# Product with V in pairs of steps, the sums leaving their bank in halves, and VectorE's remainder inside the even steps

## What is computed

```python
c_q = x @ Wq_down
c_kv = x @ Wkv_down
q_c = (c_q @ Wq_up).reshape(b, s, N_HEADS, HEAD_DIM)      # 128 heads of 4
q_r = (x @ Wq_rope).reshape(b, s, N_HEADS, ROPE)          # 128 heads of 64
k_c = (c_kv @ Wk_up).reshape(b, s, N_HEADS, HEAD_DIM)
v_c = (c_kv @ Wv_up).reshape(b, s, N_HEADS, HEAD_DIM)
k_r = x @ Wk_rope
scores = (einsum('bqhd,bkhd->bhqk', q_c, k_c) + einsum('bqhd,bkd->bhqk', q_r, k_r)) / scale
out = einsum('bhqk,bkhd->bqhd', softmax(scores), v_c)
s = out.reshape(b, s, N_HEADS * HEAD_DIM) @ Wo
...
xn = _layernorm(x)                                        # x: 8 x 256 x 512
x = x + attention(xn) * silu(ffn(xn))
```

## Time and profile before

| | us |
|---|---|
| median of 3 runs | 2015.23 |
| lowest, highest | 2010.91, 2015.4 |
| the profiled execution | 2011.28 |
| its span, first to last instruction | 2009.5 |

### The profile page before, as it was taken

How to read it: one execution, slowest core, us unless ns; L and a number is a source line. 1 busy time by engine, 2 the same in 40 slices (tenths; PEclk the granted TensorE clock), 3 DMA queues, 4 the chain that set the end, 5 groups by cost and what they waited for, 6 DMA issues and landing times.

```text
span 2009.5 us, 40807 instructions
## 1 busy us (share of the span) xinstructions
PE 1853.8 (92%) x12538; PEld 1482.1 (74%) x12538; DVE 1517.5 (76%) x1510; ACT 1410.7 (70%) x1884; POOL 1325.9 (66%) x1342
## 2 busy tenths in 40 slices
PE   8899999999999999999999999999999998888887
PEld 6677877777777777777777787777777777656665
DVE  8577787778778777877787878777777887665555
ACT  5557787777777878787877788887777776542222
POOL 5208787878777877778787878787877774032443
PEclk9999999999999999999999999999999999989888
DMA  8744444444444444444444444444444444463441
GB/s 252 218 93 104 99 108 98 102 106 102 105 106 104 101 103 98 107 96 108 97 110 95 112 97 109 97 106 97 106 99 100 107 105 112 111 170 116 137 126 63
DMA packets 186535, 225.22 MB, mean 112 GB/s; under 512 B 59710, under 2 KB 113758, under 8 KB 186462
## 3 DMA queue, kind: packets, MB, share of 16 engines
q1 hardware_dynamic: 182374, 223.52, 46.9%
q10 hardware_dynamic: 4112, 1.08, 0.3%
HBM read 61.26 MB, written 35.65 MB: 48 GB/s over the span
## 4 chain that ended last, share of the span: by engine, by line
PE 53%; DVE 14%; DMA 11%; issue 11%; ACT 5%; SPq 3%; POOL 2%; DVEq 0%; ACTq 0%; POOLq 0%
PE st L1115 14%; PE pj L1149 12%; DMA slot<-mrow 8%; PE sx L1128 7%; PE ob L1149 7%; PE ob L1081 6%; DVE pw L1019 4%; DVE mx L1026 3%; DVE slot L1037 3%; PE ap L1854 2%; ACT slot L933 1%; DMA x_raw_h<-o_scratch 1%; ACT pf L992 1%; DVE kc L1014 1%; POOL num L1515 1%
## 5 line engine op out<-in xcount | busy, mean ns | idle before, releaser
L850 POOL TENSOR_TENSOR pw<-pf,pw 128x1024 f16<-128x1024 f32 x348 | 805.6, 2330 | 306.3 <-ACT pw L1001 285.4
L1026 DVE TENSOR_REDUCE mx<-sx 128x4 fp32r<-128x1024 f32 x512 | 626.8, 1224 | 328.1 <-PE sx L1128 323.0
L992 ACT ACTIVATE pf<-st 128x1024 f32<-128x1024 f32 x464 | 446.4, 1011 | 30.8 <-PE st L1115 29.1
L1115 PE MATMUL st<-slot,k 128*128 128x512 f32 x1024 | 415.9, 406 | 45.4 <-DMA slot<-mrow 37.9
L1001 ACT ACTIVATE pw<-pf 128x1024 f16<-128x1024 f32 x348 | 355.3, 1053 | 112.1 <-PE ob L1081 99.2
L1115 PE MATMUL st<-slot,krlh 128*128 128x512 f32 x1024 | 402.7, 393 | 0.0
L1128 PEld LDWEIGHTS sx<-k,slot 88*128 88x128 f32 x2048 | 314.2, 190 | 70.9 <-issue 20.2
L1128 PE MATMUL sx<-k,slot 88*128 88x256 f32 x2048 | 332.4, 285 | 19.3 <-DMA slot<-kc 9.9
L1115 PEld LDWEIGHTS st<-slot,k 128*128 128x128 f32 x1024 | 193.2, 189 | 111.1 <-issue 71.5
L1019 DVE TENSOR_TENSOR pw<-pf,pw 128x1024 f16<-128x1024 f32 x116 | 228.2, 1967 | 1.8
L1115 PEld LDWEIGHTS st<-slot,krlh 128*128 128x128 f32 x1024 | 193.8, 189 | 35.6
(11 more groups left out here) (244 smaller groups left out, 2499.0 us busy)
## 6 DMA issues: line engine op xcount, KB each, us to landing
slot<-slot SPq DMA_DIRECT2D x256, 256.0 KB, 3.1
k<-kc SPq DMA_DIRECT2D x256, 128.0 KB
w_stage<-in_Wq_rope SPq DMA_DIRECT2D x64, 256.0 KB, 4.8
o_scratch<-o_sb SPq DMA_DIRECT2D x256, 64.0 KB
c_scratch<-stage SPq DMA_DIRECT2D x32, 256.0 KB, 3.2
c_in<-c_scratch SPq DMA_DIRECT2D x128, 64.0 KB, 2.3
k<-kc SPq DMA_DIRECT2D x128, 48.0 KB
k<-kx SPq DMA_DIRECT2D x128, 48.0 KB
```

The costliest lines, as they stand in the source:

```text
L850: nc.gpsimd.tensor_tensor(pw[:, s, kt, 1], pf[:, 2 * odd + kt], pw[:, s, kt, 0], ALU.subtract).then_inc(lo_done[kt][odd], 1)
L992: nc.scalar.activation(dst, st[:, kt], ACT.Exp, scale=SCALE).then_inc(exp_done, 1)
L1026: nc.vector.tensor_reduce(mx[:, p, lo:lo + 4], sx[:, :, :].rearrange("p a (b k) -> p (a b) k", b=2), axis=AX.X, op=ALU.max).then_inc(red_d ...
L1115: last = nc.tensor.matmul(st[:, kt, h, :].rearrange("p (e n) -> p e n", e=PH), kk, q[:, s, :, h, :], start=(n == 0), stop=(n == 1))
```

## The change

- The product with V is taken for two steps at a time, in every even step k, for the steps k-8 and k-7. It stands ahead of the whole projection of step k. Each pair fills one half of `ob`, and the transposed maxima go into the other half (`row_place`).
- The second half of the row scores stands, in even steps, ahead of the third group of the projection.
- ScalarE copies the half of a pair to `o_sb` in the same even step, between the second exponential and the roundings (`evacuate`).
- SyncE stores the two pieces of a pair in the odd step after it (kinds 1 and 3), and none in kind 2.
- VectorE's remainder of step k-5 stands between the maxima in all even steps. The low part of the content moves from between the maxima of kind 3 to the front of kind 2.
- GpSimd makes the parts of V two kinds later (kind 2), and copies them to their place in kind 3.

```diff
@@ sync
-            def store_o(at, k, pieces=(0, 1, 2, 3)):
-                bp = (k // NS) % NBP
+            def store_o(at, k):
+                bp, q = (k // NS) % NBP, (k // 2) % 2
                 g = at.g if k >= 0 else at.g - 1
-                hold(sp, passed, o_evac, at.turn(k) + 1)
-                for h, q in ((n // 2, n % 2) for n in pieces):
+                hold(sp, passed, o_evac, at.pair(k) + 1)
+                for h in range(2):
...
-                elif k % NS and at.live(k - k % NS - 5):
-                    store_o(at, k - k % NS - 5, ((), (0,), (1, 2), (3,))[k % NS])
+                elif k % 2 and at.live(k - 9):
+                    store_o(at, k - 9)
@@ gpsimd
-                    if at.split(kk):
-                        if s == 1:
-                            planes(at, kk - 1)
-                    else:
+                    if not at.split(kk):
                         whole(at, kk)
+                if s == 2 and at.live(k - 6) and at.split(k - 6):
+                    planes(at, k - 6)
+                if s == 3 and at.live(k - 7) and at.split(k - 7):
+                    kept_planes(at, k - 7)
@@ scalar
-                    if at.split(k - 4):
-                        rounded(at, k - 4)
+                if ending:
+                    if k < STEPS + 4:
+                        evacuate(at, 2 * k - 24)
+                elif k % 2 == 0 and at.live(k - 8):
+                    evacuate(at, k - 8)
+                if at.live(k - 4) and k - 4 < STEPS and at.split(k - 4):
+                    rounded(at, k - 4)
...
-                if s == 0 and at.live(k - 5):
-                    act.wait_ge(av_done, at.step(k) - 4)
-                    if at.live(k - 5 - NS):
-                        act.wait_ge(o_stored, 64 * at.turn(k - 5))
-                    nc.scalar.activation(o_sb[:, :, :], ob[:, :, :], ACT.Copy).then_inc(o_evac, 1)
+            def evacuate(at, k):
+                q = (k // 2) % 2
+                act.wait_ge(av_done, at.step(k) + 2)
+                if at.live(k - NS):
+                    act.wait_ge(o_stored[q], 32 * at.turn(k))
+                nc.scalar.activation(o_sb[:, q, :], ob[:, q, :], ACT.Copy).then_inc(o_evac, 1)
@@ vector
-                if split and k % NS == 0:
-                    remainder(at, k - 5)
+                if k % NS == (3 if at.first and k < NS else 2) and k < STEPS and at.live(k - k % NS + NS):
+                    content_lo(k // NS + 1, at.turn(k) + 1)
...
                     maxima(at, k - 1, 0)
-                    if split and k % NS == 2:
+                    if split:
                         remainder(at, k - 5)
-                    if k % NS == 3 and k < STEPS and at.live(k + 1):
-                        content_lo(k // NS + 1, at.turn(k) + 1)
                     maxima(at, k - 1, 1)
@@ tensor
+            def product(at, k):
+                v = at.step(k)
+                pe.wait_ge(exp_done, 2 * (v + 2))
...
+                if at.last and k > 2 * NS:
+                    pe.wait_ge(o_evac, at.pair(k))
+                else:
+                    pe.wait_ge(ql_done, 2 * v + 4 * NS)
+                for i in range(2):
+                    values(at, k + i)
...
-                    if c == 2 and k % NS == 0 and at.live(k - 2 * NS) and at.split(k - 2 * NS):
-                        turn(at, k - 2 * NS)
-                    if c == KD - 1 and at.live(k - 1):
+                    if c == (KD - 1 if k % 2 or not at.live(k - 2 * NS) else KD - 2) and at.live(k - 1):
                         row_scores(at, k - 1, 1)
...
-                if k % NS == 0 and at.live(k - 2 * NS) and not at.split(k - 2 * NS):
-                    turn(at, k - 2 * NS)
+                if k % 2 == 0 and at.live(k - 2 * NS):
+                    product(at, k - 2 * NS)
                 project(at, k)
```

More of the change, by code:

```diff
@@ L78, in __init__ @@
         self.o_evac = sem("o_evac")
-        self.o_stored = sem("o_stored")
+        self.o_stored = [sem(f"o_stored{q}") for q in range(2)]
+        self.lo_done = [[sem(f"lo_done{kt}{odd}") for odd in range(2)] for kt in range(2)]
         self.ql_done = sem("ql_done")
@@ L681, in attention @@
         hi_done = [[sem(f"hi_done{kt}{odd}") for odd in range(2)] for kt in range(2)]
-        lo_done = [[sem(f"lo_done{kt}{odd}") for odd in range(2)] for kt in range(2)]
+        lo_done = at_sems.lo_done
         v_step = sem("v_step")
@@ L1054, in tensor, with values @@
         def tensor(pe, head, tail):
-            def values(at, k, steps=1):
-                s, v = k % NS, at.step(k)
-                if steps:
-                    pe.wait_ge(exp_done, 2 * (v + steps))
-                    pe.wait_ge(vx_ready, v + steps)
-                    if at.split(k):
-                        for done in lo_done[0] + lo_done[1]:
-                            pe.wait_ge(done, at.pairs(k + steps - 1))
+            def product(at, k):
+                v = at.step(k)
+                pe.wait_ge(exp_done, 2 * (v + 2))
+                if at.split(k):
+                    pe.wait_ge(vx_ready, NS * (at.turn(k) + 1))
+                    for done in lo_done[0] + lo_done[1]:
+                        pe.wait_ge(done, at.pairs(k))
+                else:
+                    pe.wait_ge(vx_ready, v + 2)
                 if at.first and k == 0:
                     pe.wait_ge(vx_filled, FILLS)
-                if at.last and k == 3 * NS:
-                    pe.wait_ge(o_evac, at.turn(k))
-                elif s == 0:
+                if at.last and k > 2 * NS:
+                    pe.wait_ge(o_evac, at.pair(k))
+                else:
                     pe.wait_ge(ql_done, 2 * v + 4 * NS)
+                for i in range(2):
+                    values(at, k + i)
+            def values(at, k):
+                s = k % NS
                 for kt in range(2):
@@ L1089, in transpose_maxima @@
                 pe.wait_ge(red_done, 2 * at.step(k) + 4)
-                if k % NS and k < 3 * NS and (k > NS or not at.first):
-                    pe.wait_ge(o_evac, at.turn(k))
+                if not (at.last and k + 3 > STEPS) and at.live(k - 6):
+                    pe.wait_ge(o_evac, at.pair(k - 6) + 1)
                 if at.first and k == 0:
@@ L1182, in drain @@
                     row_scores(at, 15, 0)
-                    turn(at, 8)
+                    product(at, 8)
                     row_scores(at, 15, 1)
@@ L1398, in sync_tail @@
             sp.wait_ge(at_sems.ct_lo, NT)
-            sp.wait_ge(at_sems.o_stored, 64 * (NT - 3))
+            for q in range(2):
+                sp.wait_ge(at_sems.o_stored[q], 32 * (NT - 3))
             load_den(sp, 0)
@@ L1431, in sync_tail @@
             sp.wait_ge(at_sems.mrow_in[1], 16 * NT)
-            sp.wait_ge(at_sems.o_stored, 64 * (NT - 2))
+            for q in range(2):
+                sp.wait_ge(at_sems.o_stored[q], 32 * (NT - 2))
             load_den(sp, 1)
@@ L1481, in sync_rest @@
         sp.wait_ge(at_sems.av_done, NS * NT)
-        sp.wait_ge(at_sems.o_stored, 64 * NT)
+        for q in range(2):
+            sp.wait_ge(at_sems.o_stored[q], 32 * NT)
         for c in range(NC):
@@ L1756, in chunk @@
             if starting(c):
-                dve.wait_ge(at_sems.o_stored, 64 * NT)
+                for q in range(2):
+                    dve.wait_ge(at_sems.o_stored[q], 32 * NT)
             nc.vector.scalar_tensor_tensor(out=z[:, :], in0=zh[:, :], scalar=mk[:, 4:5], in1=zp[:, :],
```

30 lines of the change are left out of this document (16 added, 14 removed).

## The result

| | before | after |
|---|---|---|
| median of 3 runs, us | 2015.23 | 2069.09 |
| lowest, highest | 2010.91, 2015.4 | 2063.22, 2072.54 |
| the profiled execution (its span) | 2011.28 (2009.5) | 2063.22 (2061.4) |

The change makes the kernel slower: ratio 1.0275, 95% interval 1.0239 to 1.0312. Read from the first projection of one pass to that of the next, over the 14 passes of the loop, a pass takes 108.7 us instead of 105.2 (180.5 to 1702.0 us here, 176.3 to 1649.5 before).

A forecast was written before the change was run, and what follows sets the result against it. TensorE, busy nine tenths of the span, was taken as the bound. Per pass -6.5 + 7.3 + 3.1 + 0.3 = +4.2 us, +59 in 14 passes, +3 in the end passes: 2011.3 + 62 = 2073 us, range 2024 to 2112.

The forecast's parts named there:

- Removed: TensorE's waits for `mrow`, for the subtraction ahead of kind 0's product and for the maxima all go: 6.5 us per pass.
- The wait of kind 2: TensorE's product with V waits for VectorE's subtractions, now behind the content's low part: 7.3 us per pass added.
- d: Length of VectorE's content's low part, at least 1.585 us, median 1.95; kind 2's product waits d - 0.06.
- the rule: Of a two-SBUF-input VectorE instruction and a GpSimd SBUF read, the second waits for the first; 0.5 us more per pass.
- SyncE late in kind 0: A second store delays the content loads, so kind 1's row scores wait: 3.1 us per pass, 2.04 at the pass change.
- T: Start of a step's first row scores on TensorE; from kind 3's to kind 1's was put at 12.17 us.
- The split: Two products of 32 on TensorE instead of one of 64 cost a second start: 0.3 us per pass.
- The rest: ScalarE's second wait for TensorE costs 0; GpSimd's copies of V's parts end about 4 us ahead of kind 0's product.
- A: Rival: SyncE comes in time, the content loads land sooner; +1.1 us per pass, 2029 us; chance 0.14.
- B: Rival: the `mrow` wait stays, since the query copy or traffic, not the stores, delays the transfer; 2120 us; chance 0.10.
- C: Rival: VectorE is early enough that the low part fits before TensorE arrives, no kind 2 wait; 1968 us; chance 0.04.
- D: Rival: a long GpSimd instruction meets the content's low part in every turn, d 3.4 us; 2157 us; chance 0.05.

The follow-up runs named there:

- b1: Kernel before, only the stores moved: pieces 0 and 1 stored in kind 1, 2 and 3 in kind 3, none in kind 2; 2021.85 us, ratio 1.0035.
- f1: Changed kernel, with SyncE in kind 0 issuing the content loads before the loads of V and of the next content; 2011.16 us, ratio 0.9992.
- e1: Changed kernel, with the content's low part back between the maxima of kind 3; 1976.39 us, ratio 0.9815.
- e8: Changed kernel, product with V behind two projection groups, second half of the row scores ahead of the fourth group in all steps; 1976.97 us, ratio 0.9813.
- e2: Changed kernel, with the second pair's two stores moved on SyncE from kind 3 to behind the loads of kind 0; 2010.95 us, ratio 0.9978.
- e3: Changed kernel, with the content's low part of step 14 alone back between the maxima of step 15; 2023.6 us, ratio 1.005.
- b2: Kernel before, with the content's low part moved in front of kind 2 from between the maxima of kind 3; 2059.36 us, ratio 1.0232.
- e6: Changed kernel with the edits of e1 (low part back) and e2 (second pair's stores moved); 1964.16 us, ratio 0.9748.
- e9: Changed kernel with the edits of e1 (low part back) and f1 (content loads ahead of V's loads); 1954.97 us, ratio 0.9702.
- f2: Changed kernel with the edits of e9 and the product's place of e8; 1939.42 us, ratio 0.9635.

## Why the prediction was right

**The forecast.** 2073 us, which is the 2011.3 of the profiled execution before and 62 more: 4.2 more per pass and 3 at the ends. Measured are 2069, and 53.9 us more between the medians, 51.9 between the profiled executions: 3.45 more per pass and 3.6 at the ends. Direction, places of the waits and rough size came out. That the time itself is only 4 us off is in part luck: the forecast starts 4 us under the median of before, and the difference was put 8 to 10 us too high.

**Removed, forecast 6.5 us per pass: mechanism right, size 7.2.** The `mrow` transfers land in 1.8 us, as forecast, and the product of kind 0 and the maxima's transposition do not wait. The price of a wait was too low: I counted 0.16 us beyond the idle time shown, and in the earlier trace rows's turn the second of the scores behind the wait comes 0.33 us after the first instead of 0.23, so that 0.86 shown are about 1.1 lost. Another thing in the reasoning was missing: b1 shows that the terms are not additive. The `mrow` wait and the product's wait in kind 0 cover each other, and the sum was good only since the change takes both.

**The wait of kind 2, 7.3 us: mechanism right, size 5.5.** Shown are 52 waits in 52 turns. The failed term is the least d of 1.585 us. That number was the minimum of the earlier trace rows, in a trace in which a GpSimd instruction that had started earlier was still running at the start of every one of the 52 low parts. Without that it takes 1.22 us. Step 14 was to have d = 2.3 through the meeting with GpSimd's L896, and has 2.26. The three other turns were put at 1.75 and have 1.22 to 1.49. My "bound from below" was not one, and the minimum over 26 instances did not help, since every one of them had such a neighbour.

**The weighing of the rule.** The same number spoiled the verdict on the rule. The earlier trace rows was read as 1.585 + 1.20 = 2.79 against 2.28 measured, and the rule as half right. With 1.22 it is 1.22 + 1.20 = 2.42 against 2.28, and in the changed kernel 1.22 + 1.18 = 2.40 against 2.26. The Trainium skill (SBUF — State Buffer, "Who interferes with whom") says that the second to start is blocked until the first has ended. Within 0.15 us the traces agree, in f1 with the roles exchanged. In the trace of before the agreement was there to be read: each of the 52 low parts took 1.22 us plus what was left of the GpSimd instruction, less 0.14.

**SyncE late in kind 0, 3.1 us: mechanism right, size 2.5.** The waits are there, 1.7 at the change of pass (forecast 2.04) and 0.4, 0.1 and 0.3 else (0.36). The distance from T of kind 3 to T of kind 1 was put at 12.17 with a product of 32 at 0.93; the product costs 1.20 with what it does to the projection behind it, so TensorE arrives 0.25 later and waits that much less. From issue to row scores it was 2.06 us, not 2.25.

**The split, 0.3 us: too small**, 1.4. I counted a second start of 0.07. About 0.2 us are lost at every product, whatever its length: its first row starts 0.32 us after the projection ahead of it and not 0.23 (1072.68 to 1073.00 us in the trace of before), and the second product of the projection behind it comes 0.1 us late. And one of 32 takes 0.99, not half of 1.86.

**Half clock: not in the prediction**, 1.2 us per pass. I had not looked at the clock at all, since the kernel before shows none in the loop. That the sum came out better than its parts is luck: 7.3 + 3.1 + 0.3 = 10.7 added were forecast against 5.5 + 2.5 + 1.4 + 1.2 = 10.6 measured.

**The rest.** ScalarE and GpSimd are not in the list of waits, as forecast; GpSimd costs by the meeting in step 14. The ends of the program were to add 3 us and added 3.6. The turns take 26.5 and 26.0 us (26.7 forecast), the one behind the change of pass 27.7 (28.5). The turn with step 14 takes 28.8 with the half clock, 28.4 in the mean, for that and the meeting with GpSimd.

**The rivals.** A and B did not come: SyncE is late, and `mrow` lands early. e1 comes to what C describes by another way: with the low part out of the way the change is a gain, 1976 us against the 1968 of C. D did not come, since GpSimd's remainder never meets the low part in the changed kernel's loop. It does in step 2 of f1, where the low part takes up to 2.1 us in the loop, and in nearly every turn of e8, where the product stands further back and the meeting costs little.

## What to carry to other kernels

When a wait is to be removed, look which other wait of the same step ends just before it: the gain is the distance between the two, not the wait's own length, and a part that brings nothing alone can be needed for all of it. Work of an engine off the critical path is not free by its length but by its place: one instruction of 1.2 us put between a result and what waits for it cost 46 us in one order of TensorE's and 93 in the other, of 2015, and in the latter moving either of the two repaired it. A minimum duration from a trace is that of the instruction alone only if some instance stood alone; look at its neighbours before you call it a bound.

## What the runs showed of the hardware that was not expected

**The clock often falls behind a wait of about 2 us.** The lengths of the waits as shown in the trace, and the stretches with a granted clock of 0.50 (1.2 GHz) behind them:

| kernel | longest wait in the pass, us | followed by half clock, of the loop's 14 passes |
|---|---|---|
| changed kernel | 2.04 to 2.12 in 13 passes | 11 |
| b1 | 2.04 once, else 2.18 to 2.20 | 8 |
| f1 | 1.33 to 1.88 in 13 passes | 4 (behind waits of 1.76 to 1.88) |
| e2 | mostly 1.2 to 1.5 | 1 (behind a wait of 1.44) |
| before | up to 1.92 | 0 |
| e1 | up to 1.60 | 0 |
| e3 | mostly 1.5, once 1.98 | 0 |
| b2, e6, e8, e9, f2 | up to 1.67 | 0 |

Each stretch lasts 3.4 us in the records and costs 1.55 us where products of the projection stand in it (changed kernel, step 14). Behind waits under 1.7 us it came once, in e2. Above, it came in some passes and not in others with a wait of the same length, and what decides between them stays open. A wait of about 2 us can so cost more than its length: e3 took away 45 us by the waits of one step.

**Which of two instructions starts first decides who pays.** A low part of 1.22 us took 2.26 behind a GpSimd instruction that started 0.11 us ahead, and the GpSimd instruction of 1.29 us took 2.23 when it started 0.13 us behind. The first to start keeps its time; the second takes its own and what the first has left, less 0.14 us, in all 52 low parts of the trace of before.

**A small transfer is held up by larger stores issued just ahead on another engine's queue.** The row of the maxima (8 KB) lands in 1.8 us, and in up to 5.3 (before) or 5.4 us (e2) with two stores of 64 KB each just ahead of it. b1 moved only the stores, and of the 51 landings of over 4 us none was left; 5 of 102 still took 2.5 to 3.3 us.
